# Routed experts: gates from a DRAM copy, multiplied in on GpSimd

## The chip, the cores and the metric

The kernel runs on one core of a Trainium2 chip. TensorE (PE in the profile) multiplies matrices into PSUM, eight banks of 128 partitions x 512 float32; VectorE (DVE) and ScalarE (ACT) compute on PSUM and SBUF, GpSimd (POOL) on SBUF alone, and SyncE (SP) issues the DMA transfers. Each engine works through a queue of its own in order, and they meet at semaphores. The metric is the device time of one execution in microseconds, lower is better.

## What is computed

Eight layers in a row, each added to its input and normalised: four kinds of attention and four feed-forward layers. Tokens come as 4 x 512 rows of 128 channels. Only the last layer matters here:

```python
def _gate(x, w_gate):                       # E, F = (16, 64); G, TOPK_G, TOPK = (4, 2, 4)
    scores = jax.nn.sigmoid(x @ w_gate.T)
    sv = scores.reshape(T, G, E // G)
    group_scores = jax.lax.top_k(sv, 2)[0].sum(-1)
    top_groups = jax.lax.top_k(group_scores, TOPK_G)[1]
    allowed = jnp.zeros((T, G), dtype=bool).at[jnp.arange(T)[:, None], top_groups].set(True)
    masked = jnp.where(allowed[:, :, None], sv, -jnp.inf).reshape(T, E)
    _, idx = jax.lax.top_k(masked, TOPK)
    w = jnp.take_along_axis(scores, idx, axis=1)
    w = w / (w.sum(-1, keepdims=True) + 1e-06) * ROUTE_SCALE
    return (w, idx)
...
combine = (jax.nn.one_hot(idx, E, dtype=x.dtype) * weights[..., None]).sum(1)
g = jax.nn.silu(jnp.einsum('th,efh->tef', x, w1_e))
u = jnp.einsum('th,efh->tef', x, w3_e)
routed = jnp.einsum('tef,ehf,te->th', g * u, w2_e, combine)
shared = _swiglu(x, w1_s, w3_s, w2_s)
return (routed + shared).reshape(shape)
...
x = _layernorm(x + _L3_ffn_ref(x, ...), axis=-1)
```

Every expert is computed for every token, and the gate of a token and an expert (0 for 12 of the 16) scales that expert's hidden values.

## The kernel before

Each layer is a class with a `plan`, a list of steps written out by its own rule. Every engine walks the same plan and issues its part of each step, so the plan's order is the order of every queue. A class's instructions wait for the last steps of the class before. Only `Routed`, the last stage, is touched.

**Units.** The stage works on NB = 4 blocks of 512 tokens. A block has nine units (`hidden`, n = 9b + c): unit c < 8 computes experts 2c and 2c+1, which fill the 128 partitions with 2 x 64 hidden channels, and unit 8 the shared expert. Channels lie on partitions, tokens on columns. In a unit TensorE multiplies the block by two weight tiles (L2657 and L2659, banks 2(n%2) and 2(n%2)+1), ScalarE takes Silu of the first (L2790) and VectorE multiplies it by the second (L2760). The gates of the two experts must then scale 64 partitions each. They lie as 16 rows of 512 in `CT`, and a third product, L2665, with a constant 16x128 selection matrix repeats two of these rows over the partitions into bank 4 + n%2; VectorE multiplies by that (L2764) into `G9`. Unit 8 has no gate, and VectorE writes it with L2766. Two sets of banks alternate, so unit n waits for unit n-2.

**Outward.** 36 products (L2676) of `G9` with the outward weights accumulate a block in bank 6; VectorE adds the input (L2771), and `fin` normalises (L327 to L347), with one Sqrt on ScalarE.

**Gates.** For a block: `gate1` four products (L2641) and Sigmoid; `gate2` to `gate4` pick two of four groups and four of the remaining experts on VectorE with small instructions; `gate3` and `gate5` turn indices into masks and gates with `choose` (L1893), which for each of the k choices and each of four token groups issues one TENSOR_SCALAR (L1897) and, from the second choice on, one addition (L1904); `gate6` four transposes (L2648) and a copy (L2750) give `CT`.

**Order.** The plan puts all gate steps of block 0 ahead of unit 0, and those of block b+1 behind units 1 to 7 of block b, one each. `outward` and `fin` of a block stand behind the first unit of the next. In this stage GpSimd has nothing to do, and SyncE loads the selection matrix (L2799).

## Time and profile before

| | us |
|---|---|
| median of 3 timed runs | 2704.74 |
| the three runs | 2701.93 to 2707.98 |
| the profiled execution | 2712.5 |
| its span | 2710.8 |
| busy in the span: PE, DVE, ACT, POOL | 2318.9, 1637.8, 1155.7, 542.4 |

The span is the stretch that the profile covers; the profiled execution's own time is 1.7 us above it. Busy times are totals over all eight stages, which have different limits. The last stage begins at about 2524.5 in the span.

### The profile page before, as it was taken

What the parts mean: (1) busy time and instruction counts of PE and PEld (TensorE: products, weight loads), DVE (VectorE), ACT (ScalarE), POOL (GpSimd) and SP (SyncE); (2) the same over time, 40 slices, a digit from 0 to 9 for tenths busy, and PEclk for the clock granted to TensorE, in tenths of its full rate; (3) what the DMA queues carried; (4) which work ended last, traced back from release to release, by engine and by line L of the source; (5) the groups of instructions that cost most, each with busy time, mean ns of one, the idle gap of its engine ahead of it and who ended that gap; (6) DMA issues with size and microseconds to landing.
All of it is one profiled execution on the core that took longest, in us unless ns stands there. A gap on an engine that the chain in (4) does not pass through costs nothing. (4 is left out here: it accounts for less than half of the span.)

```text
span 2710.8 us, 42319 instructions
## 1 busy us (share of the span) xinstructions
PE 2318.9 (86%) x16576; PEld 1339.4 (49%) x16576; DVE 1637.8 (60%) x3368; ACT 1155.7 (43%) x1921; POOL 542.4 (20%) x671
## 2 busy tenths in 40 slices
PE   5785788888747989998996998899999999999698
PEld 2332455555514555554654343344666666565344
DVE  5564676666558777763554665122776767666555
ACT  2454455555412444444331445322654545544121
POOL 3443432333012112000000321001323232221000
PEclk7897899998958999998998899899999999999799
DMA  5210000000025323211001210000554545444000
GB/s 181 74 56 9 20 21 17 21 21 17 9 64 171 102 84 113 59 27 80 8 1 47 87 58 16 27 0 18 171 171 126 172 131 168 156 134 122 5 8 8
DMA packets 169157, 188.36 MB, mean 69 GB/s; under 512 B 47162, under 2 KB 143854, under 8 KB 164094
## 3 DMA queue, kind: packets, MB, share of 16 engines
q1 hardware_dynamic: 168958, 185.65, 22.0%
q8 instruction: 131, 2.15, 0.3%
q14 instruction: 68, 0.56, 0.1%
HBM read 85.14 MB, written 91.95 MB: 65 GB/s over the span
## 5 line engine op out<-in xcount | busy, mean ns | idle before, releaser
L928 ACT ACTIVATE AR<-PS 128x640 f32<-128x640 f32 x256 | 177.7, 704 | 223.9 <-PE PS L693 148.0
L778 DVE TENSOR_REDUCE AR<-PS 128x1 f32<-128x640 f32 x256 | 207.2, 821 | 59.6 <-PE PS L659 49.7
L1333 ACT ACTIVATE AR<-PS 128x1024 f32<-128x1024 f32 x160 | 162.3, 1024 | 157.5 <-PE PS L1182 83.6
L2499 ACT ACTIVATE AR<-PS,AR 128x512 f32<-128x512 f32 x256 | 173.7, 685 | 112.3 <-DVE AR L2432 112.1
L2432 DVE TENSOR_REDUCE AR<-PS 128x2 f32<-128x1024 f32 x128 | 156.8, 1225 | 11.1 <-DVE PS L2429 0.5
L2344 PE MATMUL PS<-AR 64*128 64x200 f32 (+2 forms) x1280 | 147.8, 358 | 2.6 <-ACT AR L2499 2.6
L2351 PE MATMUL PS<-CC,AR 128*128 128x128 f32 x1024 | 138.8, 279 | 0.9 <-DVE RA L2438 0.9
L2550 POOL TENSOR_TENSOR RA<-AR,RA 128x288 f32<-128x288 f32 x128 | 89.6, 700 | 237.4 <-ACT AR L2499 237.4
L2351 PEld LDWEIGHTS PS<-CC,AR 128*128 128x128 f32 x1024 | 113.3, 141 | 42.1 <-issue 37.3
L2344 PEld LDWEIGHTS PS<-AR 64*128 64x128 f32 x1280 | 103.5, 187 | 52.6 <-issue 43.3
L1588 PE MATMUL PS<-RA,AR 128*128 128x512 f32 x192 | 103.2, 654 | 23.6 <-ACT AR L1780 23.6
L1868 POOL TENSOR_TENSOR AR<-AR 128x1024 f32<-128x1024 f32 x32 | 75.5, 2360 | 233.2 <-DVE AR L1704 233.2
L2124 PE MATMUL PS<-AR,RA 128*128 128x512 f32 x256 | 110.2, 592 | 0.0
L1159 PE MATMUL PS<-AR 48*128 48x512 bf16 (+7 forms) x512 | 85.1, 329 | 28.0 <-DMA AR<-SP 12.3
L1269 DVE TENSOR_REDUCE AR<-PS 128x2 f32<-128x1024 f32 x64 | 77.8, 1223 | 43.1 <-PE PS L1161 42.4
L1195 PE MATMUL PS<-AR 128*32 128x512 f32 (+3 forms) x1024 | 97.7, 481 | 6.0 <-POOL AR L1394 5.2
L2429 DVE TENSOR_TENSOR PS<-PS,AR 128x288 f32<-128x288 f32 (+1 forms) x128 | 60.8, 475 | 63.8 <-PE PS L2344 59.7
L1271 DVE TENSOR_REDUCE AR<-PS 128x2 f32<-128x768 f32 x64 | 61.3, 958 | 60.9 <-PE PS L1161 60.6
L1702 DVE TENSOR_TENSOR AR<-PS,AR 128x512 f32<-128x512 f32 x64 | 43.8, 685 | 72.5 <-PE PS L1588 72.5
L708 PE MATMUL PS<-AR 128*32 128x512 f32 (+3 forms) x1024 | 83.6, 444 | 1.8 <-ACT AR L928 1.8
L1362 POOL MEMSET AR<- 128x1024 bf16 x10 | 9.0, 952 | 372.9 <-ACT XT L2067 363.2
L1178 PE MATMUL PS<-AR 51*128 51x512 bf16 (+7 forms) x512 | 75.5, 325 | 9.0 <-DMA AR<-ZM 9.0
(370 smaller groups left out, 5468.5 us busy)
## 6 DMA issues: line engine op xcount, KB each, us to landing
ZD<-RC SPq DMA_DIRECT2D x32, 1152.0 KB, 4.2
AR<-ZD SPq DMA_DIRECT2D x32, 640.0 KB
ZP<-AR SPq DMA_DIRECT2D x128, 160.0 KB, 2.6
SP<-AR SPq DMA_DIRECT2D x40, 384.0 KB, 2.6
AR<-SP SPq DMA_DIRECT2D x128, 96.0 KB
RA<-SP SPq DMA_DIRECT2D x32, 384.0 KB
SP<-AR SPq DMA_DIRECT2D x40, 256.0 KB, 2.9
RC<-RC SPq DMA_DIRECT2D x64, 130.0 KB
```

Source lines behind the costliest of these rows:

```text
L778: e.tensor_reduce(self.NMX[n // 64 % 2][:, n // 4 % 16, n % 4:n % 4 + 1], self.span(self.slots.slot[step], "scores", n), AX, ALU.max, nega ...
L928: e.activation(self.PT[m % 10][:, 0:wd], self.span(self.slots.slot[step], "turned", m), ACT.Exp).then_inc(S["s_turned"].sem, 1)
L1159: e.matmul(C.bank[2 * s + r][:, a:a + wd], QS[h, p, 128 * q:128 * q + 128], KS[h, p, 0:wd], start=True, stop=False)
L1195: i = e.matmul(b6[32 * j:32 * j + 32, 128 * kb:512], self.VP[b % 2][:, 16 * kb + 4 * (k % 4) + j, :], self.PT[at % 6][:, r, a:a + wd], sta ...
L1333: e.activation(self.PT[m % 6], C.PS[:, 2 * s:2 * s + 2, :], ACT.Exp).then_inc(S["s_turned"].sem, 1)
L1588: e.matmul(o, self.HT[:, L % NB, 64 + 128 * q:192 + 128 * q], W["wqkv" + str(L // NB)][:, 512 * x:512 * x + 512], start=True, stop=True).t ...
L2124: m = e.matmul(ba, w4[:, k, 128 * c:128 * c + 128], src[:, k, :], start=k == 0, stop=k == 3)
L2344: i = e.matmul(C.bank[2 * (n % 2) + hh][:, lo:hi], self.QT[p % 2][h, 128 * q:128 * q + 128], src[p % 2][h, lo:hi], start=True, stop=True)
L2351: i = e.transpose(o[:, 128 * k:128 * k + 128], self.PP[n % 5][:, hh, 16 + 128 * k:144 + 128 * k], C.ident)
L2432: e.tensor_reduce(self.NMX[n % 4], s, AX, ALU.max, negate=True).then_inc(S["v_scores"].sem, 1)
L2499: i = e.activation(self.PP[n % 5][:, hh, 16:528], C.bank[2 * (n % 2) + hh], ACT.Exp, bias=self.NMX[n % 4][:, hh:hh + 1], accum_out=self.DE ...
L2550: e.tensor_tensor(self.XM[p % 2][:, 2 * q:2 * q + 2, :], self.PP[n % 5][:, :, 128 * q:128 * q + 144], W["edge"].unsqueeze(1).broadcast_to( ...
```

## The change

The third product of a unit, the selection matrix, and the second VectorE multiply go. Units 0 to 7 now leave `G9` ungated. The gates, transposed and copied to `CT` as before but by ScalarE, are stored to DRAM (`send`, 16 x 512 float32) and read back by two DMA transfers (`rep`) that repeat each row over 64 partitions for all eight units at once into `GS`, 128 x 8 x 512. GpSimd then multiplies each of the eight tiles of `G9` by its part of `GS` in place (`scale`), and the outward product waits for the last of them. There are three sets of banks and of `SL`, three `G9` and two `GS`.

`choose` is replaced in both places by instructions over all token groups and choices at once: comparison, (for the gates) multiplication, and an addition or a reduction.

The plan is new as well. Unit 0 follows directly on the first gate products; gate steps 2 to 5 of block b stand behind units 5b to 5b+3, its transposes, store and replication behind unit 5b+6, and `outward` and `fin` behind units 17, 26, 33 and 35.

```diff
+        self.SL = [cv(128, 512) for _ in range(3)]
+        self.GS, self.G9 = [cv(128, 8, 512) for _ in range(2)], [cv(128, 9, 512) for _ in range(3)]
+        self.ZG = [C.dram(f"ZG{i}", (16 * 512,), F32) for i in range(2)]
...
+    def order(self):
+        plan, when = [("gate1", 0)], {}
+        for b in range(NB):
+            for i, x in enumerate(("gate2", "gate3", "gate4", "gate5")):
+                when.setdefault(5 * b + i, []).append((x, b))
+            if b + 1 < NB:
+                when[5 * b + 2].append(("gate1", b + 1))
+            when.setdefault(5 * b + 6, []).extend([("gate6", b), ("send", b), ("rep", b)])
+        for n in range(9 * NB):
+            b, c = n // 9, n % 9
+            plan.append(("hidden", n))
+            plan += when.get(n, [])
+            if b and c < 8:
+                plan.append(("scale", b - 1, c))
+            if n in (17, 26, 33):
+                b = (17, 26, 33).index(n)
+                plan += [("outward", b), ("fin", b)]
+        b = NB - 1
+        return plan + [("scale", b, c) for c in range(8)] + [("outward", b), ("fin", b)]
...
-                w.wait_ge(S["s_hidden"], n - 2)
-                e.matmul(C.bank[2 * (n % 2)], wa, x, start=True, stop=True).then_inc(th.sem, 1)
...
-                if c < 8:
-                    i.then_inc(th.sem, 1)
-                    w.wait_ge(S["v_hidden"], n - 2)
-                    w.wait_ge(S["v_gate6"], b)
-                    w.wait_ge(S["y_sel"])
-                    e.matmul(C.bank[4 + n % 2], self.SEL[:, 128 * c:128 * c + 128], self.CT[b % 2], start=True, stop=True).then_inc(th.sem, 1)
...
+            w.wait_ge(S["s_hidden"], n - 3)
+            e.matmul(C.bank[o], wa, x, start=True, stop=True).then_inc(th.sem, 1)
+            w.wait_ge(S["v_hidden"], n - 3)
+            e.matmul(C.bank[o + 1], wb, x, start=True, stop=True).then_inc(th.sem, 1)
...
+            w.wait_ge(S["v_hidden"], 9 * b + 8)
+            w.wait_ge(S["g_scale"], b, 7)
...
-                choose(e, w, C, vg, key, 0, 4, 2, [AL[:, q, :] for q in four], [self.ONE for q in four],
-                       [self.SC[:, q, 0:4] for q in four], [IF[:, q, :] for q in four])
+            e.tensor_tensor(q2, C.W["io"][:, 0:4].unsqueeze(1).unsqueeze(1).broadcast_to((128, 4, 2, 4)),
+                            IF[:, :, 0:2].unsqueeze(3).broadcast_to((128, 4, 2, 4)), ALU.is_equal).then_inc(vg.sem, 1)
+            w.wait_ge(vg, *key, part=1)
+            e.tensor_tensor(AL, q2[:, :, 0, :], q2[:, :, 1, :], ALU.add).then_inc(vg.sem, 1)
...
+            e.tensor_tensor(q4, C.W["io"].unsqueeze(1).unsqueeze(1).broadcast_to((128, 4, 4, 16)),
+                            IF[:, :, 0:4].unsqueeze(3).broadcast_to((128, 4, 4, 16)), ALU.is_equal).then_inc(vg.sem, 1)
+            w.wait_ge(vg, *key, part=1)
+            e.tensor_tensor(q4, q4, MX[:, :, 0:4].unsqueeze(3).broadcast_to((128, 4, 4, 16)), ALU.mult).then_inc(vg.sem, 1)
...
+            e.tensor_reduce(self.CM, q4.rearrange("p q i e -> p q e i"), AX, ALU.add).then_inc(vg.sem, 1)
...
-                    w.wait_ge(S["t_outward"], b - 2)
-                    e.tensor_tensor(g9[:, c, :], C.bank[4 + n % 2], gu, ALU.mult).then_inc(vh.sem, 1)
...
+            e.tensor_tensor(self.G9[n // 9 % 3][:, n % 9, :], C.bank[2 * (n % 3) + 1], self.SL[n % 3], ALU.mult).then_inc(S["v_hidden"].sem, 1)
...
+            e.activation(self.CT[b % 2], C.bank[7][0:16, :], ACT.Copy).then_inc(S["s_gate6"].sem, 1)
...
+        w.wait_ge(S["y_rep", b % 2], b)
+        w.wait_ge(S["v_hidden"], 9 * b + c)
+        e.tensor_tensor(g, g, self.GS[b % 2][:, c, :], ALU.mult).then_inc(S["g_scale"].sem, 1)
...
+                e.dma_start(self.ZG[b % 2].rearrange("(p i) -> p i", p=16), self.CT[b % 2]).then_inc(S["y_sent"].sem, 16)
...
+                z = self.ZG[b % 2].rearrange("(c e i) -> e c i", c=8, e=2)
+                for x in range(2):
+                    e.dma_start(self.GS[b % 2][64 * x:64 * x + 64], z[x].unsqueeze(0).broadcast_to((64, 8, 512))).then_inc(S["y_rep", b % 2].sem, 16)
```

TensorE at the start of the stage, before; RC holds the weights, XT the tokens and AR the scratch tiles, CC constants:

```order
L2641 MATMUL PS<-RC,XT 128x16 x3
L2648 MATMUL PS<-CC,AR 16x128 [waits v_gate5,s_gate1]
L2648 MATMUL PS<-CC,AR 16x128 x3
L2657 MATMUL PS<-XT,RC 128x512
L2659 MATMUL PS<-XT,RC 128x512
L2665 MATMUL PS<-AR 128x512 [waits y_ar,v_gate6]
L2657 MATMUL PS<-XT,RC 128x512
L2659 MATMUL PS<-XT,RC 128x512
L2665 MATMUL PS<-AR 128x512
L2641 MATMUL PS<-RC,XT 128x16 x4
```

The same place in the changed kernel (L2658 gate products, L2674 and L2676 the two products of a unit):

```order
L2658 MATMUL PS<-RC,XT 128x16 x3
L2674 MATMUL PS<-XT,RC 128x512
L2676 MATMUL PS<-XT,RC 128x512
L2674 MATMUL PS<-XT,RC 128x512
L2676 MATMUL PS<-XT,RC 128x512
L2674 MATMUL PS<-XT,RC 128x512
L2676 MATMUL PS<-XT,RC 128x512
L2658 MATMUL PS<-RC,XT 128x16 [waits s_gate1]
L2658 MATMUL PS<-RC,XT 128x16 x3
L2674 MATMUL PS<-XT,RC 128x512 [waits s_hidden]
```

The transposes, and with them the wait for block 0's gates, moved from ahead of unit 0 to behind unit 6, and the third product of each unit is gone.

VectorE around `gate3` of block 1, before:

```order
L2760 TENSOR_TENSOR AR<-PS,AR 128x512 [waits t_hidden,s_hidden]
L2764 TENSOR_TENSOR AR<-PS,AR 128x512 [waits t_hidden,v_hidden]
L1897 TENSOR_SCALAR AR<-CC,AR 128x4 [waits v_gate2]
L1897 TENSOR_SCALAR AR<-CC,AR 128x4 x7
L1904 TENSOR_TENSOR AR<-AR 128x4 [waits v_gate3]
L1904 TENSOR_TENSOR AR<-AR 128x4 x3
L2715 TENSOR_TENSOR AR<-AR 128x64 [waits v_gate3]
L2717 TENSOR_SCALAR AR<-AR 128x16 [waits v_gate3]
L2719 TENSOR_TENSOR AR<-AR 128x64 [waits v_gate3]
L2722 MAX AR<-AR 128x8 [waits v_gate3]
```

The same place now (L2769 is the unit's multiply):

```order
L2769 TENSOR_TENSOR AR<-PS,AR 128x512 [waits t_hidden,s_hidden]
L2724 TENSOR_TENSOR AR<-CC,AR 128x32 [waits v_gate2]
L2727 TENSOR_TENSOR AR<-AR 128x16 [waits v_gate3]
L2730 TENSOR_TENSOR AR<-AR 128x64 [waits v_gate3]
L2732 TENSOR_SCALAR AR<-AR 128x16 [waits v_gate3]
L2734 TENSOR_TENSOR AR<-AR 128x64 [waits v_gate3]
L2737 MAX AR<-AR 128x8 [waits v_gate3]
```

Twelve instructions for the masks became two, and one multiply of the unit is gone.

GpSimd in this stage, where before only the end of the program stood (y_fetch0 and y_fetch1 are the replications):

```order
L2818 TENSOR_TENSOR AR<-AR 128x512 [waits load_rd,g_wo,y_fetch0,s_turnx,v_hidden,v_fin,t_turnx]
L2818 TENSOR_TENSOR AR<-AR 128x512 [waits v_hidden] x7
L2818 TENSOR_TENSOR AR<-AR 128x512 [waits v_hidden,y_fetch1]
L2818 TENSOR_TENSOR AR<-AR 128x512 [waits v_hidden] x7
L2818 TENSOR_TENSOR AR<-AR 128x512 [waits v_hidden,y_fetch0]
```

Eight multiplies a block are new there, the first of each behind that block's replication.

## Rows read from the trace of the kernel before

**Rows 1.** Windows: length, busy us (instructions) per engine, granted clock, DMA share, GB/s.

```profile
2524.50:2540.70 16.20, 1.72 (x8) 1.63 (x8) 11.77 (x79) 2.79 (x3) 0.00 (x0) 0.51 0.01 5
2540.70:2546.20 5.50, 5.43 (x11) 1.95 (x11) 1.37 (x2) 0.60 (x1) 0.00 (x0) 0.59 0.00 0
...
2659.00:2704.40 45.40, 44.42 (x200) 25.50 (x198) 16.23 (x34) 9.93 (x14) 0.00 (x0) 0.98 0.02 6
```

**Rows 2.** Timeline of TensorE: start, length, line; two records make one 512-column product.

```profile
2579.31 8.30 PE L2676 MATMUL PS<-RC,AR 128*128 128x128 f32 x72
2587.45 1.02 PE L2657 MATMUL PS<-XT,RC 128*128 128x512 f32 x2
...
2594.17 1.13 PE L2657 MATMUL PS<-XT,RC 128*128 128x512 f32 x2
...
2597.14 1.13 PE L2657 MATMUL PS<-XT,RC 128*128 128x512 f32 x2
```

**Rows 3.** Groups from 2520 to the end: busy us, mean ns, idle before.

```profile
L2665 PE MATMUL PS<-AR 16*128 16x512 f32 x64 | 35.9, 640 | 0.0
...
L2760 DVE TENSOR_TENSOR AR<-PS,AR 128x512 f32<-128x512 f32 x32 | 22.0, 688 | 22.8 <-PE PS L2659 13.1 <-ACT AR L2790 9.5
L1897 DVE TENSOR_SCALAR AR<-CC,AR 128x16 f32<-128x16 f32 (+1 forms) x96 | 21.4, 287 | 0.8
L2790 ACT ACTIVATE AR<-PS 128x512 f32<-128x512 f32 x36 | 21.3, 598 | 94.0 <-PE PS L2657 93.9
...
L1904 DVE TENSOR_TENSOR AR<-AR 128x16 f32<-128x16 f32 (+1 forms) x64 | 7.8, 168 | 1.0
```

**Rows 4.** Timeline of all engines, gates of block 0: first and next after the last.

```profile
2527.90 0.21 DVE L2692 TENSOR_TENSOR AR<-AR 128x48 f32<-128x48 f32 x1 [3.19 <-ACT AR L2785]
...
2540.77 1.01 PE L2648 MATMUL PS<-CC,AR 128*16 128x128 f32 x4 [14.53 <-DVE AR L1904]
```

**Rows 5.** Timeline of TensorE in the middle expert stage.

```profile
1386.16 1.02 PE L1966 MATMUL PS<-XT,RC 128*128 128x512 f32 x2
...
1387.88 1.95 PE L1978 MATMUL PS<-RC,AR 128*128 128x128 f32 x16
```

**Rows 6.** A group of the stage, and the timeline of the kernel's end.

```profile
L2790 ACT ACT_TABLE_LOAD x7 | 9.0, 1283 | 0.1
```

```profile
2706.68 0.20 ACT L347 ACTIVATE ST<-ST 128x4 f32<-128x4 f32 x1 [10.40 <-DVE ST L335]
```

**Rows 7.** Groups of GpSimd over the whole span.

```profile
L969 POOL TENSOR_TENSOR AR<-AR 128x512 f32<-128x512 f32 x18 | 20.8, 1157 | 1.6
```

**Rows 8.** Timelines around 364 and 650, two lines' durations (min/median/max ns).

```profile
364.89 1.11 DVE L340 TENSOR_SCALAR AR<-AR 128x128 f32<-128x128 f32 x4
...
647.40 2.36 POOL L1868 TENSOR_TENSOR AR<-AR 128x1024 f32<-128x1024 f32 x1 [11.65 <-DVE AR L1704]
648.49 1.22 DVE L1731 TENSOR_TENSOR AR<-PS,AR 128x1024 f32<-128x1024 f32 x1
...
654.42 5.62 POOL L1873 TENSOR_TENSOR AR<-AR 128x1024 f32<-128x1024 f32 x3 [4.67 <-DVE AR L1718]
...
656.83 6.20 DVE L340 TENSOR_SCALAR AR<-AR 128x128 f32<-128x128 f32 x4
...
L335 DVE TENSOR_SCALAR AR<-AR x8: 169/170/782, 363.6 to 740.1; 128x4 f32<-128x4 f32 x8
...
L1772 DVE TENSOR_TENSOR YB<-XK,AR x4: 691/1044/1396, 641.0 to 757.0; 128x512 f32<-128x512 f32 x4
```

**Rows 9.** Timeline (issues, reader) and window of the nearest store and replication.

```profile
2504.50 0.84 SPq L2589 DMA_DIRECT2D ZR<-AR  x2
...
2506.41 1.09 SPq L2594 DMA_DIRECT2D RA<-ZR  x2
...
2509.78 0.69 DVE L2457 TENSOR_TENSOR AR<-PS,RA 128x512 f32<-128x512 f32 x1 [9.52 <-DMA RA<-ZR]
...
2506.40:2509.80 3.40, 0.52 (x2) 0.00 (x0) 0.02 (x1) 0.00 (x0) 0.00 (x0) 1.00 0.22 77
```

More of the change, by code:

```diff
@@ L2611, in __init__ @@
-        self.G9 = [cv(128, 9, 512) for _ in range(2)]
-        gate = lambda b: [("gate1", b), ("gate2", b), ("gate3", b), ("gate4", b), ("gate5", b, 0), ("gate5", b, 1), ("gate6", b)]
-        plan, todo = [("init",)] + gate(0), []
-        for n in range(9 * NB):
-            plan.append(("hidden", n))
-            b, c = n // 9, n % 9
-            if c == 0:
-                todo = gate(b + 1) if b + 1 < NB else []
-                if b:
-                    plan += [("outward", b - 1), ("fin", b - 1)]
-            elif todo:
-                plan.append(todo.pop(0))
@@ L2623, in __init__ @@
[L2623 removed]
+        self.SL = [cv(128, 512) for _ in range(3)]
+        self.GS, self.G9 = [cv(128, 8, 512) for _ in range(2)], [cv(128, 9, 512) for _ in range(3)]
+        self.ZG = [C.dram(f"ZG{i}", (16 * 512,), F32) for i in range(2)]
+        self.plan = self.order()
         self.parts = {
[L2625 to L2627 removed]
[4 rows of a table added]
@@ L2628, in __init__ @@
         }
         S = self.S = C.flags(self.plan, self.parts)
-        S["y_sel"] = C.flag("y_ar", [()], 16)
-        self.seven = Turns(self.plan, 1, {"gate1": S["s_gate1"], "gate6": S["v_gate6"]})
+        S["y_sent"] = C.flag("y_out", [(b,) for b in range(NB)], 16)
+        for r in range(2):
+            S["y_rep", r] = C.flag(f"y_fetch{r}", [(b,) for b in range(r, NB, 2)], 32)
+        self.seven = Turns(self.plan, 1, {"gate1": S["s_gate1"], "gate6": S["s_gate6"]})
+    def order(self):
[17 more added lines that the diff above has]
+        return plan + [("scale", b, c) for c in range(8)] + [("outward", b), ("fin", b)]
@@ new lines, in scalar, with on_scalar @@
+    def scalar(self, e, w):
+        for step in self.plan:
+            if step[0] in self.parts["s"]:
+                self.on_scalar(e, w, step)
+    def on_scalar(self, e, w, step):
+        C, S = self.C, self.S
+        kind, key = step[0], step[1:]
+        if kind == "gate1":
+            b, = key
+            w.wait_ge(S["v_gate3"], b - 1)
+            w.wait_ge(S["t_gate1"], b)
+            e.activation(self.SG.rearrange("p q e -> p (q e)"), C.bank[7][:, 0:64], ACT.Sigmoid).then_inc(S["s_gate1"].sem, 1)
+        elif kind == "gate6":
+            b, = key
+            w.wait_ge(S["y_sent"], b - 2)
+            w.wait_ge(S["t_gate6"], b)
+            e.activation(self.CT[b % 2], C.bank[7][0:16, :], ACT.Copy).then_inc(S["s_gate6"].sem, 1)
+        elif kind == "hidden":
+            n, = key
+            w.wait_ge(S["v_hidden"], n - 3)
+            w.wait_ge(S["t_hidden"], n, part=1)
+            e.activation(self.SL[n % 3], C.bank[2 * (n % 3)], ACT.Silu).then_inc(S["s_hidden"].sem, 1)
+        elif kind == "fin":
+            b, = key
+            normalise_scalar(e, w, S["v_fin"], S["s_fin"], key, C.ST[:, b % 2, :])
@@ new lines, in gpsimd, with on_gpsimd, sync @@
+    def gpsimd(self, e, w):
+        for step in self.plan:
+            if step[0] in self.parts["g"]:
+                self.on_gpsimd(e, w, step)
+    def on_gpsimd(self, e, w, step):
+        S = self.S
+        _, b, c = step
+        g = self.G9[b % 3][:, c, :]
+        w.wait_ge(S["y_rep", b % 2], b)
+        w.wait_ge(S["v_hidden"], 9 * b + c)
+        e.tensor_tensor(g, g, self.GS[b % 2][:, c, :], ALU.mult).then_inc(S["g_scale"].sem, 1)
+    def sync(self, e, w, weights):
+        S = self.S
```

263 lines of the change are left out of this document (115 added, 148 removed), and 4 rows, old and new, of the table cv.

## The prediction, made before the changed kernel ran

> **What bounds the kernel now.** Only the last of eight stages, the routed experts, is edited, so I read the whole-span numbers once and then nothing but that stage: its windows, its groups by line, the timeline of its first 17 us, one steady unit, and, for operations that it doesn't have yet, the nearest rows of other stages.
>
> The stage runs from 2524.5, when TensorE starts the gate products of the first block, to the end of the span at 2710.8: 186.3 us [rows 1]. It has three parts. From 2524.5 to 2540.7 TensorE is busy 1.72 of 16.2 us: VectorE chooses the experts of block 0, and no unit is queued ahead of that on any engine. Until 2704.4 come 36 units and four outward products. There TensorE is the bound (44.42 of the last 45.4 us) except where VectorE works on the next block's gates. The last 6.4 us are the final add, normalisation and store. A unit in steady state takes 2.97 us, from 2594.17 to 2597.14 [rows 2]: two products with the experts' weights and one, L2665, that repeats the gates over the channels. That third one is there 32 times and is busy for 35.9 us in all, 1.1 each [rows 3]. Choosing is the costliest gate work on VectorE: L1897 and L1904, 21.4 + 7.8 = 29.2 us in four blocks [rows 3]. The chain of block 0 runs 2527.90 to 2540.77, 12.9 us [rows 4]; choosing is 29.2 / 4 = 7.3 of it, the pauses between its dependent steps some 0.6 (an estimate), and the rest 5.0.
>
> **TensorE after the change.** A unit has two products left. The expert stage in the middle of the kernel issues the same pair: from 1386.16 to the outward product at 1387.88 are 1.72 us, so 0.86 a product [rows 5]. (The pair with L2665 between is spaced 0.95 to 1.0; were that spacing to stay, the 72 products would cost up to 7 us more.) The terms:
> - gate products of block 0, as now: 1.8
> - 72 products at 0.86: 61.9
> - start at the lower clock: the granted clock is 0.51 over the choosing and 0.59 over the next 5.5 us of work [rows 1], so some 4.5 us of work went by at 1.2 GHz before 2.4 GHz came back. Units now start at 1.8 us into the stage and run through that: 2.2 lost
> - three more gate products at 0.9 and four sets of transposes at 0.5: 4.7. At the lower clock the gate products took 1.72 [rows 1] and the transposes 1.01 [rows 4]; at the higher one half is left
> - four outward products, each 2579.31 to 2587.45 [rows 2], 8.14: 32.6
> - tail from the last product on, as now: 6.4
>
> Sum 109.6 if TensorE never waits. Two waits are in the plan. The last outward product needs unit 34, whose Silu stands on ScalarE behind the normalisation of block 2. From the end of the third outward product that is: add, statistics and Sqrt 2.4 (2704.4 to 2706.68, and 0.2), table load 1.28, Silu 0.6 [rows 3], multiply 0.7, GpSimd 1.2, together 6.3 with the hand-overs, against 3.4 for the two units TensorE has: 2.9 of waiting [rows 6]. And ScalarE's Sigmoid needs two table loads, 2.6 us, during which the three buffers of a unit nearly suffice: 1. That gives 113.5 us, 72.8 less than now.
>
> **VectorE after the change.** Per unit one multiply of 0.69 instead of two. The gates keep 5.0 us a block. Choosing becomes five instructions. Their price lies between 0.17 (L1904, at most 16 elements) and 0.69 (L2760, 512) [rows 3]. Between those two a line gives 1 ns an element: 0.43 each for the three of 256, 0.2 each for the two small ones, 1.7 in all. Five units with a block's gates are 3.5 + 6.7 = 10.2 us of VectorE against 8.6 + 1.4 = 10.0 of TensorE. So the two are level for the first 18 units, and whatever delays VectorE there shows at TensorE.
>
> **What delays it: GpSimd.** Each block adds eight multiplies 128x512 on GpSimd, 1.16 each by L969 [rows 7], 9.3 us a block against 25 of TensorE: no bound by itself. But the trace shows VectorE standing still behind it. At 656.83 four L340, 1.11 us in all with GpSimd idle, took 6.20 while GpSimd ran one operation after another: each waited for one GpSimd operation to end [rows 8]. A small L335, 0.17 otherwise, took up to 0.78, and L1772, an addition of two SBUF tiles, 1.40 instead of 0.69. A VectorE instruction that reads PSUM and one SBUF tile (L1731) took 1.22 beside a GpSimd operation, which for its 1024 elements is no more than the 0.69 for 512 lets expect. The Trainium skill, page "SBUF — State Buffer", section "SBUF: two separate sides", says that the two engines lock one port pair for a whole instruction, and that a VectorE operation with two SBUF inputs counts too. The trace agrees in both kinds. By the page a lock is held from whichever starts first, so it would cost GpSimd time as well; at 0.2 to 0.4 an instruction that changes the sum by less than 1.
>
> When does it bite? Gates of block 0 end at about 15.8 us into the stage. Transposes behind unit 6, ScalarE's copy and the 32 KB store bring us to 20.3: the nearest store took from 2504.50 until its reader was issued at 2506.41 [rows 9]. Replication is 2.1 MB a block in two transfers. The nearest is L2594: 256 KB landed 3.4 us after issue, at a DMA share of 0.22 and 77 GB/s; at full share that is 350 GB/s, so 6 us and some 2 us of latency, 8. It lands at 28. Then 16 GpSimd multiplies (blocks 0 and 1) run end on end, while VectorE still has the gates of block 2, the first steps of block 3, and units 11 to 17. These hold 18 instructions of the blocked kinds. Laid out in queue order 13 of them meet a GpSimd operation before unit 17 is done and wait 1.1 each, 14; 3.7 of it falls where VectorE would have waited for ScalarE. Unit 17 ends at 51.3 instead of 40.7: 10.6 us. Ends: 0 if nothing is blocked, 18.7 if 16 whole operations are paid. I take 10.6, plus 0.5 for later normalisations.
>
> **Sum.** 113.5 + 11.1 = 124.6 us for the stage, 61.7 less than 186.3. The profiled execution took 2712.5 (span 2710.8) and would take 2650.8; the median of the timed runs, 2704.74, lies 7.8 below it, so I forecast 2643. Hidden terms: the GpSimd multiplies of blocks 2 and 3 (cover: units 18 to 34, VectorE has no gates there); the gate copy moved to ScalarE, 0.6 a block in its idle time; the replication of blocks 1 to 3, 2.1 MB in each 20 us. SyncE issues only these and the stores; a store of block 0 is queued behind the last replication and has 40 us to spare. Without that cover each block pays its 8 us.
>
> The same page, section "Door 1: The DMA port swizzle", says that a transfer onto 64 partitions reaches half of the ports and that two such don't add up. By that the estimate is 218 GB/s, 9.6 + 2 us, and the sum comes out 1 lower, since GpSimd then starts when fewer gates are left.
>
> **Rivals.**
> - *Nothing is blocked.* The gate instructions are 0.2 long and might slip between GpSimd's. For it: L335 shows 0.17 in most blocks. Against: the four L340. Stage 113.5: 2632.
> - *Replication is late.* If 2.1 MB move at the 77 GB/s that L2594 shows averaged with its latency, a block takes 27 us. The four then follow each other: the stage is 20 (first store) + 6 (stores and issues between) + 4R + 9.4 (multiplies) + 8.1 + 6.4, so 50 + 4R; with R = 27 158 us and 2676, and with R = 20, where TensorE begins to wait at outward product 0, about 133 and 2651.
> - *Slower than before.* The same mechanism further on: 1024 packets of 2 KB all read one 16 KB piece of DRAM. 50 + 4R passes 186.3 at R = 34 us, 62 GB/s. At R = 37 the kernel takes 2716. Against it: L2594 has the same form, packets of 2 KB read over and over from one place, and moved 77 GB/s at a DMA share of 0.22 [rows 9].
> - *The removed product comes back as spacing.* If TensorE's products stay 0.95 apart, the blocked stretch hides most of it: 2644; with nothing blocked 2638.
>
> **How the numbers follow.** Forecast with blocking 0.62 (2636 to 2652, by the price of the GpSimd operation and of the 256-wide instructions); nothing blocked 0.20, with either spacing; late replication 0.13; slower 0.03; 0.02 that several small stalls eat the gain. The range leaves out the tail of late replication above 2664 and anything under 2628. A difference under 0.2%, 5.4 us, can't be told from none. Faster 0.95, same 0.02, slower 0.03.
>
> **What would show it.** Units 0 to 5 at once behind the first gate product; L2674 to L2676 0.86 apart; no L2665-like product; unit 17 ending near 51 us into the stage with VectorE's small two-input instructions over 1 us long between 28 and 50 us; replication landing 8 us after issue; TensorE idle 3 us ahead of the last outward product. I am wrong if TensorE waits for GpSimd ahead of outward products 0 to 2, or if those small instructions keep their 0.2.

## The result, and the profile after

The changed kernel takes 2646.61 us (median of 4 runs, 2640.60 to 2652.07), the kernel before, beside it, 2706.36 (4 runs): ratio 0.9761, 95% interval 0.974 to 0.9782. Forecast were 2643 and a range of 2628 to 2664. The profiled execution took 2652.07 us, its span 2650.4 us.

The stage in five windows. Columns: the window and its length, busy time (and instructions) of PE, PEld, DVE, ACT and POOL, granted clock of TensorE, DMA share, GB/s.

```profile
2528.10:2540.00 11.90, 11.82 (x31) 6.63 (x32) 5.86 (x40) 5.69 (x7) 0.00 (x0) 0.69 0.00 1
2540.00:2566.00 26.00, 26.00 (x83) 12.82 (x82) 22.05 (x106) 16.47 (x25) 4.39 (x4) 1.00 0.53 110
2566.00:2573.00 7.00, 2.85 (x14) 1.55 (x13) 6.79 (x23) 2.47 (x3) 5.85 (x5) 1.00 1.06 202
2573.00:2634.00 61.00, 56.69 (x285) 38.38 (x283) 30.61 (x87) 19.11 (x28) 29.78 (x24) 0.97 0.38 84
2634.00:2650.40 16.40, 9.90 (x72) 9.74 (x72) 3.40 (x15) 0.20 (x1) 0.00 (x0) 0.82 0.04 16
```

The stage runs from 2528.18 to 2650.4: 122.2 us where it was 186.3 [rows 1], 64.1 less. TensorE, busy 1.72 of the first 16.2 us before, is busy from the start. The long idle time that was not forecast is in the third window, where it is busy 2.85 of 7.00 us; a short one, 1.18 us ahead of the third transposes (2590.21), is a wait for VectorE. The beginning, and the third window, in the timeline of TensorE (start, duration, engine, line, operation, count, and the idle time ahead of it with what ended it):

```profile
2528.18 1.86 PE L2658 MATMUL PS<-RC,XT 128*128 128x16 f32 x8 [0.73 <-PE PS L353]
2529.88 2.06 PE L2674 MATMUL PS<-XT,RC 128*128 128x512 f32 x2
2531.72 1.91 PE L2676 MATMUL PS<-XT,RC 128*128 128x512 f32 x2
2533.43 1.91 PE L2674 MATMUL PS<-XT,RC 128*128 128x512 f32 x2
2535.14 1.16 PE L2676 MATMUL PS<-XT,RC 128*128 128x512 f32 x2
2536.14 1.02 PE L2674 MATMUL PS<-XT,RC 128*128 128x512 f32 x2
...
2566.74 1.02 PE L2676 MATMUL PS<-XT,RC 128*128 128x512 f32 x2
2571.91 9.93 PE L2686 MATMUL PS<-RC,AR 128*128 128x128 f32 x72 [4.14 <-POOL AR L2818]
...
2599.23 8.20 PE L2686 MATMUL PS<-RC,AR 128*128 128x128 f32 x72
...
2634.10 9.90 PE L2686 MATMUL PS<-RC,AR 128*128 128x128 f32 x72 [3.18 <-POOL AR L2818]
```

Unit 0 starts 1.7 us into the stage, and from 2536.14 on the pairs are 0.86 apart. Unit 17, whose second products start at 2566.74, is done 39.4 us into the stage, and then outward product 0 waits 4.14 us for GpSimd and takes 9.93 us instead of 8.20. SyncE's queue (L2828 is the store of a block's gates, L2835 their replication) and GpSimd's, over the same time:

```profile
2548.49 1.31 SPq L2835 DMA_DIRECT2D AR<-ZG  x2
2556.78 0.31 SPq L2828 DMA_DIRECT2D ZG<-AR  x1
2561.54 1.25 SPq L2835 DMA_DIRECT2D AR<-ZG  x2
2566.80 0.31 SPq L2828 DMA_DIRECT2D ZG<-AR  x1
2575.11 1.25 SPq L2835 DMA_DIRECT2D AR<-ZG  x2
```

```profile
2561.61 10.24 POOL L2818 TENSOR_TENSOR AR<-AR 128x512 f32<-128x512 f32 x8 [66.00 <-DMA AR<-ZG]
2574.97 9.85 POOL L2818 TENSOR_TENSOR AR<-AR 128x512 f32<-128x512 f32 x8 [3.11 <-DMA AR<-ZG]
```

The replication is issued at 2548.49, 20.3 us into the stage as forecast, and GpSimd starts 13.1 us later instead of 8. So VectorE had most of its gate work behind it. What was left shows the waiting of the forecast as soon as GpSimd runs (timeline of VectorE; ahead of 2561.61 the same lines take 0.43, 0.20 and 0.18):

```profile
2563.24 1.37 DVE L2760 TENSOR_TENSOR AR<-AR 128x256 f32<-128x256 f32 x1
...
2566.96 1.29 DVE L2705 TENSOR_TENSOR AR<-AR 128x32 f32<-128x32 f32 x1
2568.17 1.29 DVE L2706 TENSOR_TENSOR AR<-AR 128x16 f32<-128x16 f32 x1
```

In the groups by line (count, busy us, mean ns, idle time ahead) a GpSimd multiply is 1.28 us; 1.16 was assumed:

```profile
L2818 POOL TENSOR_TENSOR AR<-AR 128x512 f32<-128x512 f32 x32 | 40.0, 1284 | 98.3 <-DMA AR<-ZG 72.2 <-DVE AR L2769 26.2
```

### The profile page after: what moved, and what is told of

The parts are those of the page before. It is cut to its first block, busy times and chain, and to the rows that moved or that the text cites. A ratio compares the mean times of both kernels' runs of the same rounds, so it can differ in the third digit from the quotient of the medians.

```text
span 2650.4 us, 42030 instructions
## 1 busy us (share of the span) xinstructions
PE 2279.2 (86%) x16512; PEld 1336.5 (50%) x16512; DVE 1599.1 (60%) x3191; ACT 1157.1 (44%) x1925; POOL 581.6 (22%) x703
## 4 chain that ended last, share of the span: by engine, by line
PE 41%; DVE 5%; issue 2%; ACT 2%; DMA 2%; POOL 0%; SPq 0%; POOLq 0%; DVEq 0%; ACTq 0%
PE PS L2344 4%; PE PS L2124 4%; PE PS L2366 4%; PE PS L2351 4%; PE PS L1978 2%; PE PS L2323 2%; PE PS L1966 2%; PE PS L1968 2%; PE PS L1195 2%; PE PS L2329 1%; PE PS L2383 1%; PE PS L1178 1%; PE PS L1159 1%; PE PS L1182 1%; PE PS L2686 1%
## 5 line engine op out<-in xcount | busy, mean ns | idle before, releaser
L928 ACT ACTIVATE AR<-PS 128x640 f32<-128x640 f32 x256 | 177.7, 704 | 221.9 <-PE PS L693 146.2
L2432 DVE TENSOR_REDUCE AR<-PS 128x2 f32<-128x1024 f32 x128 | 156.8, 1225 | 11.1 <-DVE PS L2429 0.5
L1271 DVE TENSOR_REDUCE AR<-PS 128x2 f32<-128x768 f32 x64 | 61.3, 958 | 61.6 <-PE PS L1161 61.3
```

What stands on the lines that cost most here:

```text
L928: e.activation(self.PT[m % 10][:, 0:wd], self.span(self.slots.slot[step], "turned", m), ACT.Exp).then_inc(S["s_turned"].sem, 1)
L2432: e.tensor_reduce(self.NMX[n % 4], s, AX, ALU.max, negate=True).then_inc(S["v_scores"].sem, 1)
```

## The experiments

All are edits of the changed kernel, except where said. The stages ahead of the last one are the same code everywhere, yet the last stage starts between 2513.2 and 2528.2 us in the profiled executions. So the lengths of the stage are compared, from the first gate product to the end of the span. "+" is the time since that product.

| kernel | time, us | stage, us | outward products start at + |
|---|---|---|---|
| before (profiled execution) | 2712.5 | 186.3 | 54.8, 97.8, 139.8, 171.6 |
| changed (profiled execution) | 2652.07 | 122.2 | 43.7, 71.1, 91.1, 105.9 |
| changed, again (median of 5) | 2647.86 | 121.8 | 43.2, 70.9, 91.0, 105.8 |
| before + wide choosing | 2693.3 | 164.8 | 42.9, 80.6, 118.4, 150.2 |
| changed with narrow choosing | 2662.81 | 146.2 | 65.1, 95.2, 115.3, 130.1 |
| block 0's gates ahead of unit 0 | 2653.07 | 127.9 | 51.5, 76.7, 96.8, 111.6 |
| a unit's second product doubled | 2664.89 | 139.1 | 52.8, 83.6, 109.7, 124.5 |
| one column multiplied | 2635.99 | 112.1 | 39.4, 63.3, 83.4, 97.4 |
| outward 0 behind unit 20 | 2635.85 | 120.9 | 48.6, 68.5, 88.6, 103.4 |
| replication in halves | 2645.23 | 121.1 | 43.6, 70.0, 90.0, 104.8 |
| two plain loads | 2640.28 | 119.1 | 43.2, 68.0, 88.1, 102.9 |
| one plain load | 2643.49 | 122.2 | 47.9, 72.7, 92.8, 107.6 |
| multiplies later (median of 5) | 2648.43 | 124.4 | 55.2, 76.8, 92.5, 109.8 |
| one transfer, later (median of 6) | 2735.74 | 214.7 | 73.2, 114.7, 156.7, 198.5 |

Where no median is named the time is of one execution, and every stage length is of one execution. Such a length isn't sharp: the kernel with two plain loads, whose transfer takes as long as the changed kernel's, has a stage 3.1 us shorter, because its outward product 0 took 8.30 instead of 9.93 and VectorE was 0.9 less late behind it. And the last outward product, which the starts leave out, took between 8.28 and 11.11 us. So differences under some 3 us between the kernels from "outward 0 behind unit 20" to "multiplies later" show no gain or loss of the edit by themselves; the starts and waits are read instead.

The theory was that of the prediction: TensorE's own work is 113.5 us, and the rest is VectorE's two-input instructions waiting for GpSimd's. The rivals after the result: the rest is TensorE's direct wait for GpSimd, or the late transfer.

### What the parts bring

**Wide choosing alone**, in the kernel before:

```diff
...
-                choose(e, w, C, S["v_gate5"], key, 0, 16, 4, ...)
+                e.tensor_tensor(q4, C.W["io"]..., IF[:, :, 0:4]..., ALU.is_equal)
+                e.tensor_tensor(q4, q4, MX[:, :, 0:4]..., ALU.mult)
+                e.tensor_reduce(self.CM, q4.rearrange("p q i e -> p q e i"), AX, ALU.add)
```

> The kernel before with the wide choosing instructions alone: plan, third product, both multiplies and buffers as before. Block 0's gates lose 7.3 + 0.6 - 2.0 = 5.9 us on the path; in the other three blocks the stretch in which VectorE is behind (units of 4.2 us instead of 2.97, and TensorE idle 5 to 6 us ahead of the transposes) shrinks by about the same: 20 to 24 us of the 186.3. If those three are hidden after all, 6.

Measured: the stage is 164.8, 21.5 less, as expected. TensorE waits 8.75 us for block 0's gates, where it waited 14.53 [rows 4].

**Narrow choosing** in the changed kernel, the reverse edit:

> The changed kernel with the old choosing (VectorE alone, 5.9 us more a block; in it a 0.1 us memset). VectorE then has 16 us for five units against TensorE's 10 in the first 18 units: theory A, VectorE sets the pace there and the stage grows by 15 to 20 us, part of it taken in by the wait ahead of outward product 0. If choosing hides behind TensorE now, under 3 us.

Measured: 146.2, 24.0 more. The waits of TensorE that name VectorE's old chain, and the ones it causes, in the timeline:

```profile
2549.70 1.01 PE L2665 MATMUL PS<-CC,AR 128*16 128x128 f32 x4 [3.11 <-DVE AR L1904]
...
2563.75 2.08 PE L2676 MATMUL PS<-XT,RC 128*128 128x512 f32 x2 [4.22 <-DVE AR L2762]
2576.02 1.01 PE L2665 MATMUL PS<-CC,AR 128*16 128x128 f32 x4 [6.79 <-DVE AR L1904]
```

So of the 64.1 us choosing is worth 21.5 by itself and 24.0 on top of the rest; all else is worth 40.1 (186.3 - 146.2) by itself and 42.6 (164.8 - 122.2) on top. The two add up, 21.5 + 40.1 = 61.6, and 2.5 us come only together. The 15 to 20 expected here were too few: in the changed plan TensorE waits for the old chain ahead of all four transposes (2.54, 3.11, 6.79, 4.29) and in the units between (0.70, 4.22), 21.7 us.

**Block 0's gates ahead of unit 0**, the rest of the plan as it is:

```diff
-        plan, when = [("gate1", 0)], {}
+        plan, when = [("gate1", 0), ("gate2", 0), ("gate3", 0), ("gate4", 0), ("gate5", 0), ("gate6", 0), ("send", 0), ("rep", 0)], {}
...
```

> The changed kernel with all gate steps of block 0, its store and its replication ahead of unit 0, as before the change; the rest of the plan stays. TensorE then idles from the gate products to the transposes: Sigmoid 1.5 + gates 6.7 + about 1, so unit 0 starts some 11 us into the stage instead of 1.7, at the lower clock. Theory A: 9 to 10 us more at the start, 5.9 fewer at outward product 0, since the replication is then long done: 126 us. If the early start is worth its full length, as in a stage without that wait: 132.

Measured: 127.9, 5.7 more, nearer the 126 of theory A than 132. TensorE stands still for 8.70 us behind the gate products, and 3.0 of that come back on balance: the wait ahead of outward product 0 is gone, but GpSimd now starts 27.0 us into the stage, and TensorE waits 1.88 and 0.91 us for VectorE in the units of that time.

**The second product doubled**, on units 0 to 7 of a block: 32 products more, 32 x 0.86 = 27.5 us.

```diff
             e.matmul(C.bank[o + 1], wb, x, start=True, stop=True).then_inc(th.sem, 1)
+            if c < 8:
+                e.matmul(C.bank[o + 1], wb, x, start=True, stop=True)
```

> The changed kernel with the second product of units 0 to 7 of each block issued twice into the same bank, 32 products more, on TensorE alone. If the third product of before was on the path, this gives its time back: 32 x 0.86 = 27.5 us, less the 5.9 of waiting and lower clock ahead of outward product 0 that longer units take in: 144 us. If VectorE or the replication set the pace, less than half of it, under 134 us.

Measured: 139.1, only 16.9 more, between the 144 and the 134 of the two expectations. Outward product 0 (2576.85) starts right behind a pair (2575.99), without a wait. So 27.5 - 16.9 = 10.6 us of what the changed kernel loses are covered once TensorE has more to do; that this is the loss around GpSimd is an argument here, and the next run measures it.

### What GpSimd costs

**One column multiplied.** GpSimd's 32 operations, their waits and the transfers stay, but each takes one column of 512, so gating is left out for the others:

```diff
-        e.tensor_tensor(g, g, self.GS[b % 2][:, c, :], ALU.mult)
+        e.tensor_tensor(g[:, 0:1], g[:, 0:1], self.GS[b % 2][:, c, 0:1], ALU.mult)
```

> The changed kernel; each GpSimd multiply covers one column of 512 instead of all (the other columns stay without their gates). Every wait stays. Theory A (the trace of the changed kernel): TensorE loses time only where it waits for the last multiply of a block, 4.1 us ahead of outward product 0 and 3.2 ahead of product 3, and by the lower clock behind each of these waits (9.9 instead of 8.2 us a product); VectorE's blocked instructions cost it 1 to 2 us. Then the stage, 122.2 us, loses 4.1 + 1.8 + 1.2 at products 0 and unit 21, and 1.2 at the end: 114 us, and no VectorE instruction over 0.6 us but the multiplies. Theory B (the forecast's): VectorE blocked by GpSimd costs 10 us; then the stage falls to 110 or less.

Measured: 112.1, 10.1 less than 122.2. That lies between the 114 of theory A and the 110 of theory B, and by itself decides for neither. VectorE's lines in groups by line, first of the changed kernel, then of this one:

```profile
L2760 DVE TENSOR_TENSOR AR<-AR 128x256 f32<-128x256 f32 x4 | 3.6, 898 | 0.1
L2705 DVE TENSOR_TENSOR AR<-AR 128x32 f32<-128x32 f32 x4 | 1.9, 469 | 0.0
```

```profile
L2760 DVE TENSOR_TENSOR AR<-AR 128x256 f32<-128x256 f32 x4 | 1.7, 425 | 0.1
L2705 DVE TENSOR_TENSOR AR<-AR 128x32 f32<-128x32 f32 x4 | 0.8, 196 | 0.0
```

And its outward product 0 starts right behind unit 17:

```profile
2560.77 1.02 PE L2676 MATMUL PS<-XT,RC 128*128 128x512 f32 x2
2561.63 8.20 PE L2686 MATMUL PS<-RC,AR 128*128 128x128 f32 x72
```

The differences of the outward starts split the 10.1 us: 4.3 ahead of outward 0; 3.4 up to outward 1, of which 1.7 is the longer product (9.93 for 8.20) and 1.7 VectorE being late; nothing up to outward 2; 0.8 ahead of outward 3, and 1.6 in it (9.90 for 8.28). So in the changed kernel as it stands 8.4 us are TensorE's own waits for GpSimd and the slower products behind them, and only 1.7 come through VectorE.

**Outward product 0 behind unit 20.** If its wait were all, putting three units ahead of it would win it back.

```diff
-            if n in (17, 26, 33):
-                b = (17, 26, 33).index(n)
+            if n in (20, 26, 33):
+                b = (20, 26, 33).index(n)
```

> The changed kernel with outward product 0 behind unit 20 instead of unit 17; nothing else. Theory A: the wait of 4.1 us ahead of it and the 1.8 us of lower clock go, the stage takes 116 to 117 us instead of 122.2. Theory B: units 18 to 20 now stand among VectorE's blocked gate instructions and are late by what the wait was; 121 to 123 us.

Measured: 120.9, where theory A said 116 to 117 and theory B 121 to 123. No wait ahead of outward products 0 to 2, but units 18 to 20, which now come while GpSimd works, are the ones that are late:

```profile
2557.41 1.78 PE L2676 MATMUL PS<-XT,RC 128*128 128x512 f32 x2 [2.21 <-DVE AR L2769]
```

The direct wait and the blocking stand in for each other, if not in full: TensorE waits for GpSimd, or for a VectorE that waits for GpSimd. Outward product 3 starts 2.5 us earlier than in the changed kernel (103.4 for 105.9), and then takes 11.11 us instead of 9.90.

**Replication in halves**: four tiles each, so that GpSimd starts sooner.

```diff
-                for x in range(2):
-                    e.dma_start(self.GS[b % 2][64 * x:64 * x + 64], z[x]...)
+                for h in range(2):
+                    for x in range(2):
+                        e.dma_start(self.GS[b % 2][64 * x:64 * x + 64, 4 * h:4 * h + 4], z[x][4 * h:4 * h + 4]...)
```

> The changed kernel; each block's replication comes as two halves of four units each, with a semaphore each, so GpSimd starts 5 to 6 us earlier. Theory A: the wait ahead of outward product 0 nearly goes (4.1 + 1.8), 117 us. Theory B: GpSimd's multiplies now fall among the gates of block 2 and units 12 to 16, VectorE's two-input instructions there take 1.3 us each, about ten of them, and unit 17 ends 5 to 10 us later than 39.4 into the stage: 122 us or more.

Measured: 121.1, nearer the 122 of theory B than 117. GpSimd starts 7.8 us after the first issue (2542.53 to 2550.36), the wait ahead of outward product 0 is gone, and it starts at +43.6 all the same: unit 17 is 4.2 us later. The rows of VectorE in between show why:

```profile
2552.94 1.17 DVE L2728 TENSOR_TENSOR AR<-AR 128x16 f32<-128x16 f32 x1
2554.14 1.24 DVE L2731 TENSOR_TENSOR AR<-AR 128x64 f32<-128x64 f32 x1
2555.41 1.13 DVE L2733 TENSOR_SCALAR AR<-AR 128x16 f32<-128x16 f32 x1
```

### Why the transfer takes 13 us, and what a fast one would bring

**Two plain loads**: the same two transfers of 1 MB onto 64 partitions, but from distinct DRAM rows, so no piece is read over and over; GpSimd multiplies by weights, not by gates.

```diff
-                    e.dma_start(self.GS[b % 2][64 * x:64 * x + 64], z[x].unsqueeze(0).broadcast_to((64, 8, 512)))...
+                    e.dma_start(self.GS[b % 2][64 * x:64 * x + 64], self.C.A["rc"][64 * x:64 * x + 64, 0:4096]...)
```

> The changed kernel; the two replicating transfers read 128 different rows of 16 KB from a weight tensor in DRAM instead of one 16 KB piece over and over (so the tiles are multiplied by other numbers than the gates). Size and destination are the same. If reading one place repeatedly is what makes 2.1 MB take 13.1 us from issue to the first multiply instead of the 8 forecast, this takes 7 to 8. If the way onto the partitions or the packets' number does, 12 to 13. The stage: 4 us fewer, or the same.

Measured: 12.9 us from issue to the first multiply (2539.60 to 2552.45). Repeated reading isn't the cause. (The stage of 119.1 is not the transfer's doing, see behind the table.)

**One plain load** of the same 2 MB onto all 128 partitions, again other numbers than the gates:

```diff
-                for x in range(2):
-                    e.dma_start(self.GS[b % 2][64 * x:64 * x + 64], z[x]...)
+                e.dma_start(self.GS[b % 2], self.C.A["rc"][:, 0:4096]...)
```

> The changed kernel, but the 2.1 MB that GpSimd multiplies by come in one plain transfer over 128 partitions from distinct rows of DRAM, not in two over 64 partitions each; what is multiplied is other numbers than the gates. Theory A (two transfers on 64 partitions each do not add up their halves of the ports): 7 to 8 us from issue to the first multiply, in place of 13.1 (changed kernel) and 12.9 (two plain transfers). Theory B (the time is that of the bytes, about 160 GB/s whatever the partitions): 12 to 13 us. With 7 to 8 us the first multiply starts near +28 and the wait ahead of outward product 0 gives way to blocked gate instructions, so the stage stays at 119 to 122 us; with 12 to 13 us it is 119 to 122 with the wait of 3 to 4 us.

Measured: 7.9 us. SyncE's queue and GpSimd's:

```profile
2539.58 0.37 SPq L2834 DMA_DIRECT2D AR<-in_rc  x1
```

```profile
2547.46 16.32 POOL L2818 TENSOR_TENSOR AR<-AR 128x512 f32<-128x512 f32 x13 [58.86 <-DMA AR<-in_rc]
```

The windows of the transfers say what is halved (first the changed kernel, then this one; the last two numbers are DMA share and GB/s):

```profile
2549.00:2561.00 12.00, 12.00 (x38) 5.92 (x37) 10.90 (x64) 8.31 (x12) 0.00 (x0) 1.00 0.88 178
```

```profile
2540.00:2547.00 7.00, 7.00 (x20) 3.07 (x19) 6.21 (x30) 4.97 (x7) 0.00 (x0) 1.00 0.81 301
```

As many DMA engines are busy (0.88 and 0.81 of 16), but one moves 178 / 14.1 = 12.6 GB/s in the one and 301 / 13.0 = 23.2 in the other. The middle of each transfer, without its ends, shows it more sharply:

```profile
2552.00:2559.00 7.00, 7.00 (x26) 3.65 (x25) 6.38 (x30) 3.38 (x7) 0.00 (x0) 1.00 1.05 201
```

```profile
2542.00:2545.00 3.00, 3.00 (x9) 1.33 (x8) 2.31 (x9) 2.40 (x4) 0.00 (x0) 1.00 0.98 412
```

This run differs from the one before in two things, the number of transfers and the partitions of each, and no run separates them. The row that the forecast was priced by, L2594, has the form of the changed kernel's replication: two transfers onto 64 partitions each, of 128 KB. In half microseconds its middle, in the kernel before, is

```profile
2507.90:2508.40 0.50, 0.00 (x0) 0.00 (x0) 0.00 (x0) 0.00 (x0) 0.00 (x0) 1.00 0.54 189
2508.40:2508.90 0.50, 0.00 (x0) 0.00 (x0) 0.00 (x0) 0.00 (x0) 0.00 (x0) 1.00 0.59 205
```

It already moves the 200 GB/s that the large transfers move, at a DMA share of 0.59 instead of 1.05. More share brought no more bytes. Why the share is lower at the same rate, the traces don't say.

And the stage has not become shorter, 122.2: GpSimd's 13 multiplies in a row now meet the gates of blocks 2 and 3, and 12 VectorE instructions in 17 us stand behind it, from L2724 to L2705:

```profile
2549.28 0.72 DVE L2724 TENSOR_TENSOR AR<-CC,AR 128x32 f32<-128x32 f32 x1
2550.03 1.17 DVE L2727 TENSOR_TENSOR AR<-AR 128x16 f32<-128x16 f32 x1
...
2561.28 1.37 DVE L2760 TENSOR_TENSOR AR<-AR 128x256 f32<-128x256 f32 x1
```

This is the plan as it was predicted, with the 8 us of the forecast: outward product 0 at +47.9 without a wait for GpSimd, where 51.3 was forecast. With one column multiplied it starts at +39.4, so blocking costs 8.5 us here.

### Two attempts at a better plan

**Multiplies later.** If GpSimd starts only when VectorE has no gates left, nothing is blocked.

```diff
-            if n in (17, 26, 33):
+            if n in (23, 27, 31):
...
+        w.wait_ge(S["v_gate5"], NB - 1)
```

> The changed kernel with two edits: GpSimd's first multiply waits until the gates of block 3 are done (so no multiply runs while VectorE has gate work or the units up to 18), and the outward products stand behind units 23, 27, 31 and 35 instead of 17, 26, 33 and 35. Theory A (VectorE's blocked instructions and the wait ahead of the first outward product, with the fall of the clock behind it, are what GpSimd costs, 4.3 + 1.7 + 1.9 of the 10.1 us between the changed kernel and the one with one column scaled): unit 17 ends near +39.4, the gate instructions of blocks 2 and 3 keep 0.2 to 0.4 us, TensorE does not wait ahead of outward products 0 to 2, and up to 3.2 us ahead of the last: stage 113 to 116 us, 6 to 9 us less than the 122.2 of the changed kernel, about 2639 us. Theory B (the 32 multiplies are late whenever they start, because 41 us of them now have to fit between about +42 and the end): 42 + 41 + the last outward product and tail, 15, stay below 113 only if nothing separates them; if they are held up by the units' own instructions the stage is 120 us or more, no faster than the changed kernel.

> The changed kernel itself, timed on the same chip for the comparison: stage 122 us, outward products at about +44, 71, 91 and 106 us, the first behind a wait of 4 us for GpSimd; first multiply 13 us after the replication is issued. Theory A of the run before expects this one to be 6 to 9 us slower than it, theory B equal.

Measured on one chip, beside 2710.93 for the kernel before: 2648.43 and 2647.86, ratios 0.9777 (0.9761 to 0.9794) and 0.9774 (0.9758 to 0.9789). No gain, as theory B had it, and the stage is 124.4 against 121.8. One half of theory A holds: L2705 and L2760 keep 197 and 425 ns. The other half fails at a number. The release was put at +40, where TensorE is at unit 17; but VectorE trails it, and its last gate instruction ends at +45.2:

```profile
2562.97 19.63 POOL L2819 TENSOR_TENSOR AR<-AR 128x512 f32<-128x512 f32 x16 [76.59 <-DVE AR L2763]
```

TensorE wants block 0 at +50.0 and gets it at +55.2: it waits 5.14 us, and the two outward products behind that take 11.23 and 8.99 instead of 8.20.

**One transfer, later.** The same with the outward products where the multiplies should be ready, and the replication as one transfer over 128 partitions, for which the gates lie in DRAM in another order:

```diff
-            if n in (23, 27, 31):
+            if n in (26, 30, 33):
...
-                e.dma_start(self.ZG[b % 2].rearrange("(p i) -> p i", p=16), self.CT[b % 2])...
+                e.dma_start(self.ZG[b % 2].rearrange("(e c i) -> c e i", c=8, e=2), self.CT[b % 2])...
...
-                z = self.ZG[b % 2].rearrange("(c e i) -> e c i", c=8, e=2)
-                for x in range(2):
-                    e.dma_start(self.GS[b % 2][64 * x:64 * x + 64], z[x].unsqueeze(0).broadcast_to((64, 8, 512)))...
+                z = self.ZG[b % 2].rearrange("(e j) -> e j", e=2)
+                e.dma_start(self.GS[b % 2].rearrange("p c i -> p (c i)"), z.unsqueeze(1).broadcast_to((2, 64, 4096)))...
```

> The whole computation, with three edits of the changed kernel. The gates lie in DRAM in another order, so that one transfer over 128 partitions repeats them instead of two over 64 each; GpSimd's first multiply waits for the gates of block 3, as in the run with the multiplies later; and the outward products stand behind units 26, 30, 33 and 35 instead of 23, 27, 31 and 35. In that earlier run GpSimd was released at +45.4, not at +40 (VectorE had the gates and unit 18 done only at +45.2), and so block 0 was ready at +55.2, 5.1 us after TensorE wanted it. Theory A (the time lost there is waiting and the lower clock behind it, 5.1 + 3.0 + 0.8, and the waits go when the outward products stand where the multiplies are ready): unit 26 ends at about +55.2, so there is no wait above 0.5 us ahead of outward product 0, none ahead of 1 and 2, 3.2 us ahead of the last, each of the first three takes 8.2 us, and the stage is 95.5 + 3.2 + 9.9 + 6.4 = 115 us (113 to 118), 4 to 8 us less than the 121.8 and 122.2 of the changed kernel: about 2641, ratio to the kernel before 0.975. The replication of block 0 lands 8 us after issue. Theory B (what is not waited for ahead of outward product 0 is paid later, since GpSimd's multiplies of blocks 2 and 3 then come too late): the waits ahead of outward products 2 and 3 grow to 5 us or more and the stage is 120 us or more, ratio 0.977 or above.

Measured: 2735.74 us, ratio 1.0091 (1.0075 to 1.0107), 0.9% slower than the kernel before. Neither theory foresaw it. The transfer, expected to take 8 us, takes 42 (chain of the work that ended last, in order of time: start, duration, what):

```profile
2535.51 42.17 DMA AR<-ZG
2579.24 8.61 POOL AR L2819 x7
2587.84 31.55 issue
2619.42 9.80 POOL AR L2819 x8
```

The window of the first transfer shows a DMA share of 0.13 and 53 GB/s:

```profile
2536.00:2577.00 41.00, 30.70 (x87) 14.09 (x85) 23.63 (x119) 14.18 (x22) 0.00 (x0) 0.91 0.13 53
```

0.13 of 16 DMA engines is 2.1, and each moves 25 GB/s, about as fast as in the one plain load (23.2). So two engines carried everything. The source's pattern begins with a dimension of two, the two experts. That this is the reason isn't separated from the new order in DRAM by a run of its own; the Trainium skill, page "DMA: Bandwidth & Descriptors", section "Why a DMA increments its semaphore by 16 and not by 1", states it: the number of engines is the largest up to 16 that divides the slowest dimension of both patterns, here two. The trace agrees. A form with the repetition of 64 outermost was not tried, so whether the late plan beats the changed kernel is open.

## Why the prediction was right, and where it was not

**Sum.** Forecast for the stage were 124.6 us, measured 122.2 and 121.8; forecast for the kernel 2643, measured 2646.61. The profiled execution was forecast at 2650.8 and took 2652.07. Its stage was 2.4 shorter than forecast, and the stages ahead of it, which are unchanged, 3.7 longer than in the profiled execution of before; the median lies 5.5 below it, not 7.8.

**TensorE, 113.5.** Right. The kernel with one column multiplied, where L2705 and L2760 keep their 0.2 and 0.43 us, takes 112.1; the 1 us put down for ScalarE's Sigmoid doesn't show in it, as TensorE's one idle time there is the 2.39 ahead of the last outward product. Spacing is 0.86, the lower clock lasts until 2535.14, 7.0 us into the stage, and costs 2.8 (from 2529.88 to 2536.14 are 6.26 us for four steps of 0.86), forecast 2.2; the wait ahead of the last outward product is 3.18, forecast 2.9. Not in the sum was that an outward product behind a wait may take 9.9 us instead of 8.2, with the granted clock at 0.82 in the last 16.4 us; it happens twice, 3.3 us.

**VectorE.** Right: five choosing instructions take 0.18 + 0.17 + 0.42 + 0.43 + 0.58 = 1.78 us a block, forecast 1.7. The two kernels with choosing swapped put 21.5 to 24.0 us on it.

**Replication, 8 us: the step that failed.** It took 13.1. The row it was priced by, L2594 [rows 9], was the right one in form. What failed is the scaling: 77 GB/s at a DMA share of 0.22 was taken to mean 350 GB/s at full share. In its middle the same row moves 189 to 205 GB/s at 0.54 to 0.59, and the replication moves 201 at 1.05: the rate was at its end before the share was. 350 is near what one transfer on 128 partitions moves (301 over 7 us, 412 in the middle), and that one takes 7.9 us. In the prediction the Trainium skill's page "SBUF — State Buffer", section "Door 1: The DMA port swizzle", stood against the row with 9.6 + 2 us; by the runs the page's rule is right in kind, and 11.6 is still 1.5 too low. (That two such transfers don't add up stands on the same page in the section "Can I just issue two DMAs to hit both halves?".) That the later start would take 1 off the sum isn't borne out: with the landing after 7.9 us the stage is 122.2 as well.

**Blocking, 11.1: the mechanism is real, but in the changed kernel it brings only a small part, and that the sum came out is in part luck.** The lines named do wait for one GpSimd operation each, 0.2 becoming 1.1 to 1.3. But unit 17 ends at 39.4, not 51.3: GpSimd started 5 us later, and ahead of the end of unit 17 VectorE waited out a whole operation in one of these instructions, L2760, not in 13. Instead TensorE waited for GpSimd itself, which the text had named as the sign of being wrong, as it was about the place. In all, GpSimd costs 10.1 us (122.2 - 112.1), near the 11.1, but 8.4 of them are TensorE's waits and the slower products behind them, and 1.7 blocking. With the transfer of the forecast, in the one-load run, the step does what was forecast: 12 instructions were blocked where 13 were laid out, and unit 17 is 8.5 us later (47.9 for 39.4), so the 10.6 was 2.1 too high, and the 40.7 for unit 17 without blocking 1.3 too high. The runs with outward 0 later, with halves and with one load show why the sum didn't notice: each of them removes the wait ahead of outward product 0, and pays in blocked instructions, 120.9, 121.1 and 122.2.

**Rivals.** *Nothing blocked* falls by L2705 and its neighbours; its 113.5 is what the one-column kernel shows. *Spacing* falls: 0.86. *Late replication* came in part, 13.1 instead of 27. *Slower than before* was not the changed kernel's fate, but its formula was measured by accident: the stage is 50 + 4R, and with R = 42 it should be 218; it is 214.7. The four replications are issued 42.4, 41.7 and 42.0 us apart there, each behind the landing of the one before, which is the chain that the formula has. The text gave 2716 at R = 37, which at 4 us for each makes 2736 at 42; that 2735.74 was measured is closer than the stage, 3.3 us off, gives reason for. A transfer that keeps two DMA engines busy is all that it takes.

## What to carry over

A GpSimd operation of 1.3 us next to a VectorE that is level with TensorE costs TensorE either way, as a wait or through blocked VectorE instructions; moving the start of one or the consumer of the other trades them. In these runs only less GpSimd work removed the loss; whether a late start with a fast transfer does was not reached. A transfer's rate isn't its share scaled up to 1: look at the middle of the nearest row in short windows, and take the rate that it holds there. And bring a large tile in one transfer over all partitions, with many rows in the outermost dimension of both patterns: 2 MB took 7.9 us as one transfer onto 128 partitions, 13.1 as two onto 64, and 42 where the source's pattern began with a dimension of two. A total that comes out doesn't confirm its terms: here 11.1 of blocking stood against 1.7, and a wait of another kind filled the gap. When an engine is to start behind another, read the release from that engine's own timeline, not from where TensorE stands in the plan.
